# Key units by halves of the batches, and state products directly behind the second own terms, in a one-core decoder block

## The chip, the core and the metric

The kernel runs on one core of a Trainium2 chip. The metric is the device time of one launch in microseconds (us). It has five engines with an instruction stream each: TensorE (PE in the profile, with its weight loads as PEld), VectorE (DVE), ScalarE (ACT), GpSimd (POOL) and SyncE (SP, which here only issues DMAs; SPq in the profile). They are kept in step by semaphores alone: a wait in one engine's stream holds everything behind it on that engine.

## The reference

The input x has 16 sequences of 64 tokens and 256 features, all in float32, and there is a context of 16 x 64 x 128. The block is three layers, each with its residual and a LayerNorm:

```python
# 1: recurrent attention, 16 heads of 16, in 4 chunks of 16 tokens; per chunk, with state S
kh = k @ S;  v_new = gradient of a LayerNorm loss at kh
o  = q + LN(q @ S - tril(q k^T) eta v_new);  S = S - (k eta)^T v_new
x  = LN(x + (rmsnorm(o * sigmoid(gate)) * norm_w) @ Wo)
# 2: cross attention, 16 heads of 128
q = rmsnorm(x @ Wq) * gq;  k = rmsnorm(ctx @ Wk) * gk
x = LN(x + softmax(q k^T / sqrt(128)) @ (ctx @ Wv) @ Wo)
# 3: gated feed-forward with rows rounded to 8 bit
x = LN(x + quant(silu(quant(x) @ Wg) * (quant(x) @ Wu)) @ quant(Wd))
```

## The kernel before

The program has three parts in time. The first prepares weights and projections. The second is the recurrence: chunks c = 0 to 3, each in halves h = 0, 1 (a half is 8 of the 16 heads). The third is a pipeline over 8 tiles of 128 tokens that does the output projection of the recurrence, the cross attention and the feed-forward; its steps are numbered from i = -2.

**The recurrence.** For each chunk PE runs, for both halves: `state_products(c, h)` (L518, k and q times the state; it waits for `s_ready`), `scores_ttt(c, h)` (L500, q k^T within the chunk; made one chunk ahead, it waits for the masked keys `kb` and its half 1 ends with `a_done`), and `own_terms(c, h)` (L528, it waits for `ub_ready`, the update rows of that half, and for `at_ready`, the masked scores). Each is 64 matmuls of 32 rows, which the trace shows as 128 pairs of a weight load and a matmul. Below they are called state(c,h), scores(c,h) and own(c,h). DVE does in order: `state_read(c, 0)` (begins with the transpose khR, L1427), `kb_rows` and `a_masked` (ak, L1409 and L1414), the previous chunks' outputs (`output_inverse`, ors, L1525, which waits for a root osd on ACT; `out_c`), `chain(c, 0)` (some 12 small steps that end with ub, L1462), `state_read(c, 1)`, `output_sums`, `output_inverse`, `chain(c, 1)`, `out_normed`, `after_own_terms(c, 0)` (qhR, L1513, and the new state rows st, L1517, which set `s_ready`), `out_gated`, and `after_own_terms(c, 1)`. ACT takes roots (`state_root`, `output_root`, L1080), squares and the masked keys (`k_blocks`, L1013).

**The key units.** The keys of the cross attention, which need only the context, are made in between: 32 units, each one head of one half of the batches (512 columns). A unit is one float32 matmul on PE (L659, two pairs in the trace) into bank 6 or 7, a square (L1071) and a scaled copy (L1073) on ACT. After every fourth unit PE sums four squares into bank 5 (L650, `key_sum`, 8 pairs), each into one row of its own. When all 32 are summed, ACT takes one root `krow` (L1076), SP writes it to DRAM and reads it back with one row per batch and head (`roots_to_rows`, L420 and L423, both halves), DVE inverts it (`key_scales`, kinv, L1549), SP writes it (`scales_out`, L427) and reads it back as the broadcast rows `rkb` (`scale_rows(i)`, L435), with which DVE multiplies the scores of tile i (`scores_out`, pr, L1707). `rkb` lies over buffers of the key units, so it is loaded after all of them.

A unit's place is set by hand, by the numbers in `KEY_PLACES`, one list for each chunk; PE takes a number at each place between its recurrence steps, and ACT takes the same numbers in its own order:

```python
# PE, chunk c: state(c,0) keys state(c,1) keys scores(c+1,0) keys own(c,0) keys scores(c+1,1) keys own(c,1) keys
# ACT, chunk c:
keys(places[0])
if c < NCH - 1:
    k_blocks(c + 1)
keys(places[1])
output_root(2 * c - 1)
state_root(c, 1)
```

Bank 6 and 7 alternate, so unit n waits until ACT has emptied unit n - 2. Behind the last sums PE runs 8 matmuls that are not used (`warm(4, 8)`, L643) and then `ttt_out(0)` (L834), the first of the pipeline, whose result DVE reads (rw, L1757).

Of the kernel before, what the change touches and what calls it, by code (L numbers as in the profile page):

```python
# [32 lines left out]
ACT = mybir.ActivationFunctionType  # L33
# [5 lines left out]
NCH = T // C  # L39
# [16 lines left out]
KEY_PLACES = [(1, 2), (2, 2, 1, 1, 2, 1), (2, 2, 1, 1, 2, 1), (2, 3, 3, 3)]  # L56
# [3 lines left out]
def decoder_block(nc, x, ctx_in, Wq, Wk, Wv, Wo, Wbeta, ln_w, ln_b, Wg1, Wg2, norm_w,  # L60
                  XWq, XWk, XWv, XWo, gq, gk, w1_in, w2_in, out):
    stack = ExitStack()
    with stack:
# [213 lines left out]
        def unit_of(n):  # L277
            return n % 2, n // 4 * 2 + n % 4 // 2
# [100 lines left out]
        def _(sp):  # L379
# [64 lines left out]
            load_x()  # L444
            sp.wait_ge(sem("og_ready"), 2)
# [11 lines left out]
            scale_rows(1)  # L457
            scales_out(1)
# [13 lines left out]
        def _(pe):  # L472
# [372 lines left out]
            warm(4, 8)  # L845
# [3 lines left out]
            pe.wait_ge(sem("k_rooted"), 1)  # L849
# [101 lines left out]
        def _(act):  # L951
# [113 lines left out]
            def key_unit(n):  # L1065
# [8 lines left out]
                else:  # L1074
                    act.wait_ge(sem("k_summed"), NKU)
# [875 lines left out]
```

## Time and profile before

| | us |
|---|---|
| median of 3 runs | 381.57 |
| lowest and highest | 378.9, 383.26 |
| the profiled execution | 382.47 |
| its span | 380.7 |
| PE busy in the span | 344.8 (91%) |
| DVE busy | 264.5 (69%) |
| ACT busy | 201.3 (53%) |

The profiled execution is longer than its span by 1.77 us, which lies outside the first and the last instruction. Its time is 0.9 us over the median of the runs and inside their spread. In the rows of a timeline the first number is the start in us from the begin of the span, the second the time from the first to the last of the merged instructions, the bracket at the end the time that the engine was idle just before, and what released it ("issue": nothing that the profile shows).

### The profile page before, as it was taken

The numbers are of one execution on the slowest core, as the hardware profiler recorded it, in microseconds if no ns is written. First come the engines' busy times: TensorE is split into PE (matmuls) and PEld (weight loads), VectorE is DVE, ScalarE is ACT, GpSimd is POOL, SyncE is SP. The second block draws the span as 40 slices with busy tenths as digits, with TensorE's granted clock in tenths as the row PEclk, the third lists the DMA queues.
The fourth block names the chain that finished last, engine by engine and source line by source line (L and its number), as shares of the span: only waits on it lengthen the run. The fifth ranks groups of instructions, "written<-read, shape, count | busy, mean of one in ns | idle before, by whom it ended". The sixth has DMA issues, their size and how long they took to land.

```text
span 380.7 us, 11631 instructions
## 1 busy us (share of the span) xinstructions
PE 344.8 (91%) x5095; PEld 242.8 (64%) x5098; DVE 264.5 (69%) x536; ACT 201.3 (53%) x371; POOL 75.6 (20%) x91
## 2 busy tenths in 40 slices
PE   1999997998979877998999999999999999999974
PEld 1544585455435332587698796896977969866731
DVE  0499997897797899556263674855846739566795
ACT  1245974855525635255516556555555566576351
POOL 3009300000000000000062341522714505300100
PEclk9999999999987968999999999999999999999998
DMA  8997000000402001029120100200201000000000
GB/s 195 277 289 248 4 4 3 5 3 23 151 4 83 34 2 58 16 53 203 31 57 0 50 8 15 58 0 16 57 1 56 16 15 0 2 15 0 16 1 28
DMA packets 17986, 19.96 MB, mean 52 GB/s; under 512 B 3712, under 2 KB 15376, under 8 KB 17680
## 3 DMA queue, kind: packets, MB, share of 16 engines
q1 hardware_dynamic: 17328, 18.69, 18.8%
q8 instruction: 40, 0.66, 0.8%
q10 hardware_dynamic: 608, 0.54, 0.7%
q14 instruction: 10, 0.08, 0.1%
HBM read 18.04 MB, written 1.18 MB: 50 GB/s over the span
## 4 chain that ended last, share of the span: by engine, by line
PE 73%; DVE 15%; ACT 4%; issue 3%; DMA 3%; SPq 0%; POOLq 0%; POOL 0%; DVEq 0%
PE ps L790 14%; PE ps L724 12%; PE ps L547 6%; PE ps L659 5%; PE ps L782 5%; PE ps L767 4%; PE ps L500 3%; PE ps L809 2%; PE ps L528 2%; PE ps L740 2%; PE ps L518 2%; PE ps L617 2%; PE ps L650 2%; PE ps L758 2%; DMA xn<-in_x_dram 2%
## 5 line engine op out<-in xcount | busy, mean ns | idle before, releaser
L724 PEld LDWEIGHTS ps<-x1t,xwq 128*128 128x128 f32 x512 | 59.2, 192 | 6.4 <-issue 4.2
L724 PE MATMUL ps<-x1t,xwq 128*128 128x128 f32 x512 | 62.1, 278 | 0.7 <-ACT x1t L1188 0.7
L790 PE MATMUL ps<-mvo,cxp 128*128 128x256 f32 x224 | 51.8, 383 | 0.5 <-ACT cxp L1199 0.5
L1893 POOL TENSOR_SCALAR rstd<-mv 128x1 f32<-128x1 f32 x20 | 4.4, 218 | 212.6 <-DVE mv L1635 212.6
L790 PEld LDWEIGHTS ps<-mvo,cxp 128*128 128x128 f32 x224 | 41.3, 190 | 6.6 <-ACT cxp L1199 0.8
L659 PE MATMUL ps<-ctxt,xwk 128*128 128x512 f32 x64 | 39.1, 727 | 3.5 <-ACT kt L1073 2.3
L1151 ACT ACTIVATE qt<-ps 128x512 f32<-128x512 f32 x32 | 19.1, 596 | 33.9 <-PE ps L724 33.9
L1071 ACT ACTIVATE ksq<-ps 128x512 f32<-128x512 f32 x32 | 18.9, 591 | 21.4 <-PE ps L659 13.4
L1073 ACT ACTIVATE kt<-ps,gks 128x512 f32<-128x512 f32 x32 | 21.9, 683 | 0.0
L1158 ACT ACTIVATE qsq<-ps 128x512 f32<-128x512 f32 x32 | 19.0, 593 | 4.2 <-PE ps L740 4.2
L659 PEld LDWEIGHTS ps<-ctxt,xwk 128*128 128x128 f32 x64 | 11.9, 217 | 14.3 <-ACT kt L1073 6.2
L528 PEld LDWEIGHTS ps<-ak,ub 32*32 32x32 f32 x1024 | 11.9, 109 | 13.7 <-issue 13.5
L767 PEld LDWEIGHTS ps<-kt,qt 128*64 128x64 f32 x512 | 16.2, 138 | 6.8 <-ACT qt L1151 3.8
L528 PE MATMUL ps<-ak,ub 32*32 32x48 f32 (+1 forms) x1024 | 13.4, 200 | 6.9 <-DVE ub L1462 3.5
L1644 DVE TENSOR_SCALAR x<-rr,mv,rstd 128x256 f32<-128x256 f32 x16 | 6.6, 412 | 18.7 <-POOL rstd L1894 18.5
L782 PE MATMUL ps<-pt,ctx 64*128 64x512 f32 x64 | 18.5, 638 | 0.7 <-ACT pt L1178 0.7
L767 PE MATMUL ps<-kt,qt 128*64 128x64 f32 x512 | 18.4, 225 | 0.0
L1707 DVE TENSOR_TENSOR pr<-ps,rkb 128x1024 f32<-128x1024 f32 x8 | 9.8, 1224 | 12.2 <-PE ps L767 8.7
L1199 ACT ACTIVATE cxp<-ps 128x512 f32<-128x512 f32 x28 | 15.3, 606 | 4.5 <-PE ps L782 4.5
L1683 DVE TENSOR_TENSOR gs<-ps,s 128x352 f32<-128x352 f32 x16 | 8.3, 522 | 13.4 <-PE ps L809 13.2
L1908 POOL TENSOR_TENSOR rq<-rq,mhalf 128x16 f32<-128x16 f32 x6 | 17.4, 2908 | 0.5
L500 PEld LDWEIGHTS ps<-kqi,kb 32*32 32x32 f32 x1024 | 10.1, 110 | 7.8 <-issue 6.8
(238 smaller groups left out, 683.2 us busy)
## 6 DMA issues: line engine op xcount, KB each, us to landing
rkb<-kscale SPq DMA_DIRECT2D x16, 256.0 KB, 4.2
ctx<-in_ctx_dram SPq DMA_DIRECT2D x4, 512.0 KB, 8.7
xwo<-in_L_xattn_Wo_dram SPq DMA_DIRECT2D x1, 2048.0 KB, 14.2
xwq<-in_L_xattn_Wq_dram SPq DMA_DIRECT2D x4, 512.0 KB, 4.8
w1n<-in_L_ffn_w_gate_up_dram SPq DMA_DIRECT2D x1, 1408.0 KB, 9.9
xwv<-in_L_xattn_Wv_dram SPq DMA_DIRECT2D x1, 1024.0 KB, 11.2
xwk<-in_L_xattn_Wk_dram SPq DMA_DIRECT2D x1, 1024.0 KB, 16.5
xn<-in_x_dram SPq DMA_DIRECT2D x2, 512.0 KB, 5.9
```

Of the source, the lines that this page charges most:

```text
L500: last = mm(ps[part, 4 * BANK + g * C:4 * BANK + (g + 1) * C], kb[part, g * 32:(g + 1) * 32], kq[part, col:col + C], start=True, stop=True)
L528: last = mm(ps[part, g * GW + C:g * GW + C + w], ub[part, g * 32:(g + 1) * 32], ak[part, g * (C + 32):g * (C + 32) + w], start=c == 0 and ...
L547: last = mm(bank(bk), w[:, k * D + hh * P:k * D + (hh + 1) * P], xt[:, k * B * T + half * BANK:k * B * T + (half + 1) * BANK], start=k == ...
L659: mm(bank(6 + n % 2), xwk[:, h * XD:(h + 1) * XD], ctxt[:, half * BANK:(half + 1) * BANK], start=True, stop=True)\
L724: last = mm(bank(n % 2, P, t * P), xwq[qn][:, k * BANK + t * P:k * BANK + (t + 1) * P], x1t[:, (i % 2) * D + k * P:(i % 2) * D + (k + 1) * ...
L767: last = mm(ps[b2 * T:(b2 + 1) * T, 4 * BANK + h * T:4 * BANK + (h + 1) * T], qt[:, h * P + b2 * T:h * P + (b2 + 1) * T], kt[:, (i * XH + ...
L782: turn_done(mm(bank(bk), ctx2[rows, b * CD:(b + 1) * CD], pt[rows, :].rearrange("p (h q) -> p h q", q=P)[:, :, b2 * T:(b2 + 1) * T], start ...
L790: last = mm(bank(turn_banks[turn_of[("y", i, 0)]], D), context_of(i)[:, h * P:(h + 1) * P], mvo[:, h * D:(h + 1) * D], start=h == 0, stop= ...
L1071: A(ksq[n % 4][:, :], bank(6 + n % 2), ACT.Square).then_inc(sem("k_squared"), 1)
L1073: A(o, bank(6 + n % 2).rearrange("p (i t) -> p i t", t=P), ACT.Copy, scale=gks[:, 1:2]).then_inc(sem("key_emptied"), 1)
L1151: A(qt[:, qn * BANK:(qn + 1) * BANK], bank(n % 2), ACT.Copy).then_inc(sem("q_copied"), 1)
L1158: A(qsq[:, (n % 2) * BANK:(n % 2 + 1) * BANK], bank(n % 2), ACT.Square).then_inc(sem("q_squared"), 1)
```

## The change

It has four parts. The order of the key units goes from alternating halves of the batches to all 16 heads of the first half and then the second. The root is taken twice: after unit 17 for the first half, and at the end; the rows of the first half go through DRAM at a place of SP's stream behind `load_x`, their inverse is taken by DVE in the last chunk's output steps (`key_scales(0)`), and `scale_rows(0)` no longer stands behind the inverse of both. In the recurrence, scores(c,1) is moved from before own(c-1,1) to after state(c,0), own(c,1) is followed by state(c+1,0) with no unit between, and `a_masked` stands behind `out_c` on DVE. The 8 matmuls of `warm` are 3.

```diff
-KEY_PLACES = [(1, 2), (2, 2, 1, 1, 2, 1), (2, 2, 1, 1, 2, 1), (2, 3, 3, 3)]
+KEY_PLACES = [(1, 2), (1, 2, 2, 1, 3), (1, 1, 2, 1, 4), (1, 2, 2, 3, 3)]
...
         def unit_of(n):
-            return n % 2, n // 4 * 2 + n % 4 // 2
+            return divmod(n, XH)
...
             def roots_to_rows(half):
-                sp.wait_ge(sem("k_rooted"), 1)
-                for odd in range(2):
-                    at = 64 * half + 32 * odd
...
-                sp.wait_ge(sem("k_rows_out"), 32 * (half + 1))
+                sp.wait_ge(sem("k_rooted"), half + 1)
+                for q in range(4):
+                    at = 32 * q + 4 * half
...
+                sp.wait_ge(sem("k_rows_out"), 64 * (half + 1))
+                sp.wait_ge(sem("kh_done"), 4)
...
@@ key_sum
                 pe.wait_ge(sem("k_squared"), n + 1)
-                at = 31 - h // 2
+                if half == 1:
+                    pe.wait_ge(sem("k_rooted"), 1)
+                at = 31 - h // 4 - 4 * half
...
@@ PE, the loop over chunks
                 state_products(c, 0)
                 keys(next(places))
+                if c >= 2:
+                    scores_ttt(c, 1)
+                keys(next(places))
                 state_products(c, 1)
                 keys(next(places))
                 if c < NCH - 1:
                     scores_ttt(c + 1, 0)
                     keys(next(places))
                 own_terms(c, 0)
-                if c < NCH - 1:
-                    keys(next(places))
-                    scores_ttt(c + 1, 1)
                 keys(next(places))
                 own_terms(c, 1)
-                for n in places:
-                    keys(n)
+            keys(next(places))
...
-            warm(4, 8)
+            warm(4, 3)
...
-            pe.wait_ge(sem("k_rooted"), 1)
+            pe.wait_ge(sem("k_rooted"), 2)
@@ ACT, key_unit
+                if n == XH + 1:
+                    act.wait_ge(sem("k_summed"), XH)
+                    A(krow[:, :], bank(5), ACT.Sqrt, bias=eps_t[:, 1:2], scale=1.0 / XD).then_inc(sem("k_rooted"), 1)
@@ ACT, the loop over chunks
-                keys(places[0])
+                keys(places[0] + places[1])
                 if c < NCH - 1:
                     k_blocks(c + 1)
-                keys(places[1])
+                    keys(places[2] + places[3])
+                else:
+                    keys(places[2])
                 output_root(2 * c - 1)
                 state_root(c, 1)
@@ DVE
                     kb_rows(c)
-                    a_masked(c)
                     output_inverse(2 * c - 2)
                     out_c(c - 2)
+                    a_masked(c)
...
             output_sums(2 * NCH - 2)
+            key_scales(0)
             last_scale(qhR, 0)
...
                     last_out(2)
-                    key_scales()
+                    key_scales(1)
```

On PE, from own(1,0) to state(2,0), before:

```order
L528 MATMUL ps<-ak,ub 32x48 x63
L659 MATMUL ps<-ctxt,xwk 128x512 [waits key_emptied]
...
L500 MATMUL ps<-kqi,kb 32x16 x64
L659 MATMUL ps<-ctxt,xwk 128x512 [waits key_emptied] x2
L528 MATMUL ps<-ak,ub 32x48 [waits ub_ready,kbr_ready,at_ready]
L528 MATMUL ps<-ak,ub 32x48 x63
L659 MATMUL ps<-ctxt,xwk 128x512 [waits key_emptied]
L518 MATMUL ps<-kqi,st 32x64 [waits s_ready]
```

and in the changed kernel (own terms are L529 there, units L663, state products L519, scores L501, sums L653):

```order
L529 MATMUL ps<-ak,ub 32x48 x63
L663 MATMUL ps<-ctxt,xwk 128x512 [waits key_emptied] x3
L529 MATMUL ps<-ak,ub 32x48 [waits ub_ready,kbr_ready,at_ready]
L529 MATMUL ps<-ak,ub 32x48 x63
L519 MATMUL ps<-kqi,st 32x64 [waits s_ready]
L519 MATMUL ps<-kqi,st 32x64 x63
```

The 64 score matmuls of half 1 and the unit ahead of the state products are gone from here; the scores stand behind state(2,0) and unit 12 now, and in chunk 1 the sums of units 4 to 7 stand before own(1,0).

On ACT, chunk 1 from the masked keys to the roots osd and sdc that DVE waits for (each pair of ksq and kt is a unit), before, units 5 and 6:

```order
L1013 ACTIVATE kb<-kqi,mask_h 128x32x16
L1071 ACTIVATE ksq_130<-ps 128x512 [waits k_summed,key_done]
L1073 ACTIVATE kt<-ps,gks 128x4x128
L1071 ACTIVATE ksq_131<-ps 128x512 [waits k_summed,key_done]
L1073 ACTIVATE kt<-ps,gks 128x4x128
L1080 ACTIVATE osd<-ovs,eps_t 128x32 [waits ovs_ready]
```

and in the changed kernel, units 6, 7 and 8 (squares L1074, copies L1076, roots L1087):

```order
L1016 ACTIVATE kb<-kqi,mask_h 128x32x16
L1074 ACTIVATE ksq_131<-ps 128x512 [waits k_summed,key_done]
L1076 ACTIVATE kt<-ps,gks 128x4x128
L1074 ACTIVATE ksq_74<-ps 128x512 [waits k_summed,key_done]
L1076 ACTIVATE kt<-ps,gks 128x4x128
L1074 ACTIVATE ksq_129<-ps 128x512 [waits k_summed,key_done]
L1076 ACTIVATE kt<-ps,gks 128x4x128
L1087 ACTIVATE osd<-ovs,eps_t 128x32 [waits ovs_ready]
```

The roots of chunk 1 stand behind unit 8 where they stood behind unit 6; those of chunk 2 stand behind unit 16 where they stood behind unit 15.

On SP, from the last weight load to the second half's rows, before:

```order
L381 DMA xwq_160<-in_L_xattn_Wq_dram 128x2x512 [waits mg_done]
L420 DMA kroot<-krow 8x8x64 [waits k_rooted]
...
L423 DMA kinv<-kroot 128x64 [waits k_rows_out]
L427 DMA kscale<-kinv 128x64 [waits k_inverted,k_summed]
L435 DMA rkb<-kscale 64x1024 [waits k_scales_out]
L435 DMA rkb<-kscale 64x1024
L381 DMA ctx_58<-in_ctx_dram 64x16x128 x2
L435 DMA rkb<-kscale 64x1024 [waits k_scales_out]
L435 DMA rkb<-kscale 64x1024
L427 DMA kscale<-kinv 128x64 [waits k_inverted]
```

and in the changed kernel:

```order
L428 DMA kscale<-kinv 128x64 [waits k_inverted]
L436 DMA rkb<-kscale 64x1024 [waits k_scales_out,k_summed]
L436 DMA rkb<-kscale 64x1024
L381 DMA ctx_58<-in_ctx_dram 64x16x128 x2
L436 DMA rkb<-kscale 64x1024 [waits k_scales_out]
L436 DMA rkb<-kscale 64x1024
L420 DMA kroot<-krow 4x8x64 [waits k_rooted]
L420 DMA kroot<-krow 4x8x64 x3
L424 DMA kinv<-kroot 128x64 [waits kh_done,k_rows_out]
L428 DMA kscale<-kinv 128x64 [waits k_inverted]
```

The second half's rows go out and come back behind the loads of rkb for tiles 0 and 1 and of the context, where before they went ahead of them.

## Rows read from the trace of the kernel before

**Rows 1.** Busy time by stretches: from:to, length, then each engine's busy us, clock, DMA

```profile
100.00:120.00 20.00, 17.55 (x613) 10.20 (x616) 18.31 (x48) 9.96 (x20) 0.00 (x0) 0.83 0.02 4
...
240.00:280.00 40.00, 40.00 (x340) 34.12 (x340) 27.81 (x54) 23.08 (x40) 17.66 (x16) 1.00 0.12 31
```

**Rows 2.** Timeline of DVE, chunk 1 and the start of chunk 2

```profile
82.08 0.35 DVE L1525 RECIPROCAL ors<-osd 128x32 f32<-128x32 f32 x1 [0.39 <-ACT osd L1080]
...
87.96 0.48 DVE L1462 TENSOR_SCALAR ub<-us__111,mask_h 128x128 f32<-128x128 f32 x2
...
93.25 0.45 DVE L1513 STREAM_TRANSPOSE qhR<-ps 128x256 f32<-128x256 f32 x1 [1.68 <-PE ps L528]
...
97.25 0.45 DVE L1427 STREAM_TRANSPOSE khR<-ps 128x256 f32<-128x256 f32 x1 [2.23 <-PE ps L518]
```

**Rows 3.** Timeline of PE, chunks 1 and 2

```profile
75.85 1.99 PE L518 MATMUL ps<-kqi,st 32*32 32x64 f32 x128
77.77 1.98 PE L659 MATMUL ps<-ctxt,xwk 128*128 128x512 f32 x4
79.68 1.26 PE L500 MATMUL ps<-kqi,kb 32*32 32x16 f32 x128
...
91.31 1.82 PE L528 MATMUL ps<-ak,ub 32*32 32x48 f32 x128
...
96.77 0.42 PE L518 MATMUL ps<-kqi,st 32*32 32x64 f32 x15 [0.85 <-issue]
...
105.97 0.44 PE L500 MATMUL ps<-kqi,kb 32*32 32x16 f32 x31 [0.63 <-issue]
...
111.34 0.71 PE L528 MATMUL ps<-ak,ub 32*32 32x48 f32 x42 [1.82 <-issue]
111.98 2.08 PE L659 MATMUL ps<-ctxt,xwk 128*128 128x512 f32 x2
```

**Rows 4.** Table of the costliest groups: the two ACT operations of a key unit

```profile
L1071 ACT ACTIVATE ksq<-ps 128x512 f32<-128x512 f32 x32 | 18.9, 591 | 21.4 <-PE ps L659 13.4
L1073 ACT ACTIVATE kt<-ps,gks 128x512 f32<-128x512 f32 x32 | 21.9, 683 | 0.0
```

**Rows 5.** Timeline of DVE, chunk 2 and the start of chunk 3

```profile
110.18 0.35 DVE L1525 RECIPROCAL ors<-osd 128x32 f32<-128x32 f32 x1 [0.39 <-ACT osd L1080]
...
120.83 0.45 DVE L1513 STREAM_TRANSPOSE qhR<-ps 128x256 f32<-128x256 f32 x1 [1.16 <-PE ps L528]
...
124.70 0.45 DVE L1427 STREAM_TRANSPOSE khR<-ps 128x256 f32<-128x256 f32 x1 [2.10 <-PE ps L518]
```

**Rows 6.** Timeline of ACT and PE behind the last sums

```profile
153.62 0.69 ACT L1076 ACTIVATE krow<-ps,eps_t 128x512 f32<-128x512 f32 x1 [0.77 <-PE ps L650]
...
155.26 1.89 PE L834 MATMUL ps<-wo,ogt 128*128 128x256 f32 x8
```

**Rows 7.** Timeline of the first scores: inverse, loads, scores, root table, exponential

```profile
165.69 0.91 DVE L1549 RECIPROCAL kinv<-kinv 128x128 f32<-128x128 f32 x1
...
168.16 1.12 SPq L435 DMA_DIRECT2D rkb<-kscale  x2
...
170.71 3.63 SPq L435 DMA_DIRECT2D rkb<-kscale  x2
171.09 1.15 PE L767 MATMUL ps<-kt,qt 128*64 128x64 f32 x32
...
173.15 1.23 DVE L1707 TENSOR_TENSOR pr<-ps,rkb 128x1024 f32<-128x1024 f32 x1 [3.56 <-DMA rkb<-kscale]
...
176.72 1.28 ACT L1208 ACT_TABLE_LOAD   x1
...
178.41 1.06 ACT L1208 ACTIVATE pr<-pr 128x1024 f32<-128x1024 f32 x1 [0.40 <-DVE pr L1718]
```

**Rows 8.** Lines 427 (stores kscale<-kinv) and 423 (loads kinv<-kroot): time to landing

```profile
DMA to landing us min/median/max: 1.5/4.9/8.3
...
DMA to landing us min/median/max: 1.8/2.5/3.1
```

More of the change, by code:

```diff
@@ L416, in roots_to_rows @@
             def roots_to_rows(half):
-                sp.wait_ge(sem("k_rooted"), 1)
-                for odd in range(2):
-                    at = 64 * half + 32 * odd
-                    sp.dma_start(kroot[half].rearrange("b (r o) t -> o r b t", o=2)[odd],
-                                 krow[at:at + XH // 2, :].rearrange("p (b t) -> p b t", t=T)).then_inc(sem("k_rows_out"), 16)
-                sp.wait_ge(sem("k_rows_out"), 32 * (half + 1))
-                sp.dma_start(kinv[:, half * T:(half + 1) * T], kroot[half].rearrange("b h t -> (b h) t")).then_inc(sem("k_roots_in"), 16)
+                sp.wait_ge(sem("k_rooted"), half + 1)
+                for q in range(4):
+                    at = 32 * q + 4 * half
+                    sp.dma_start(kroot[half].rearrange("b (r o) t -> o r b t", o=4)[q],
+                                 krow[at:at + 4, :].rearrange("p (b t) -> p b t", t=T)).then_inc(sem("k_rows_out"), 16)
+                sp.wait_ge(sem("k_rows_out"), 64 * (half + 1))
+                sp.wait_ge(sem("kh_done"), 4)
+                sp.dma_start(kinv[:, half * T:(half + 1) * T], kroot[half].rearrange("b h t -> (b h) t")).then_inc(sem("k_roots_in%d" % half), 16)
             def scales_out(half):
-                sp.wait_ge(sem("k_inverted"), 1)
+                sp.wait_ge(sem("k_inverted"), half + 1)
                 sp.dma_start(kscale[half * B // 2:(half + 1) * B // 2, :].rearrange("b (h t) -> (b h) t", t=T),
@@ L444, in _ @@
             load_x()
+            roots_to_rows(0)
             sp.wait_ge(sem("og_ready"), 2)
@@ L457, in _ @@
             scale_rows(1)
+            roots_to_rows(1)
             scales_out(1)
@@ L646, in key_sum @@
                 half, h = unit_of(n)
-                rows = slice(64 * half + 32 * (h % 2), 64 * half + 32 * (h % 2) + 32)
+                rows = slice(32 * (h % 4), 32 * (h % 4) + 32)
                 pe.wait_ge(sem("k_squared"), n + 1)
-                at = 31 - h // 2
-                mm(bank(5)[rows, :], onehot[:, at:at + 32], ksq[n % 4][:, :], start=h < 2, stop=h >= XH - 2).then_inc(sem("k_summed"), 1)
+                if half == 1:
+                    pe.wait_ge(sem("k_rooted"), 1)
+                at = 31 - h // 4 - 4 * half
+                mm(bank(5)[rows, :], onehot[:, at:at + 32], ksq[n % 4][:, :], start=n < 4, stop=n >= NKU - 4,
+                   skip_group_check=True).then_inc(sem("k_summed"), 1)
             def key_unit(n):
@@ L1116, in _ @@
                 output_square(c - 1)
-                keys(places[0])
+                keys(places[0] + places[1])
                 if c < NCH - 1:
                     k_blocks(c + 1)
-                keys(places[1])
+                    keys(places[2] + places[3])
+                else:
+                    keys(places[2])
                 output_root(2 * c - 1)
                 state_root(c, 1)
-                for n in places[2:-2]:
-                    keys(n)
-                keys(places[-2])
+                keys(places[4] if c < NCH - 1 else places[3])
                 gated_square(c - 1)
-                if c < NCH - 1:
-                    keys(places[-1])
             last_root(0)
@@ L1545, in out_c, with key_scales @@
                 V.transpose(o, oR[:, :]).then_inc(sem("o_feat"), 1)
-            def key_scales():
-                dve.wait_ge(sem("k_roots_in"), 32)
-                V.reciprocal(kinv[:, :], kinv[:, :]).then_inc(sem("k_inverted"), 1)
+            def key_scales(half):
+                own = kinv[:, half * T:(half + 1) * T]
+                dve.wait_ge(sem("k_roots_in%d" % half), 16)
+                V.reciprocal(own, own).then_inc(sem("k_inverted"), 1)
             kb_rows(0)
```

7 lines of the change are left out of this document (3 added, 4 removed).

## The prediction

> **What bounds the kernel now.** I read the busy times by stretches first, then the timeline of DVE through the recurrence, then PE's around every point at which DVE was idle. From 200 us on PE is busy all the time (40.00 of 40 us), and nothing of the change is there; what it can move lies before. In the recurrence no engine is full: in 100 to 120 us DVE has 18.31 us of work and PE 17.55, at a granted clock of 0.83 of full [rows 1]. The steps of DVE are one behind another, so I take DVE's stream as the path, and PE counts where DVE waits for it. Such waits stand twice in each of chunks 1 and 2: for own(c,1) 1.68 and 1.16 us, and for the next state(c+1,0) 2.23 and 2.10 us [rows 2, 5]. Together 7.2 us, and the most that the new order can give there.
>
> **PE's stops.** PE waits also for nothing that the profile shows: 0.85, 0.63 and 1.82 us in the middle of a group [rows 3]. Counting the pairs of a weight load and a matmul between the first two stops (the last 15 of state(2,0), unit 12 with sums, unit 13, state(2,1), units 14 and 15, 97 of scores(3,0)) gives 15 + 2 + 8 + 2 + 128 + 4 + 97 = 256; to the third it is 127. So the places are marks every 128 pairs, and PE stops where it reaches one too soon. The mark before 96.77 lies 116 pairs into own(1,1), by its row at 91.31 + 0.9 x 1.82 = 92.95 us; my estimate is thus 3.8 us from mark to mark, with 5.4 (105.97 to 111.34) as the other end. The new order puts own(c,1) and state(c+1,0) together, 256 pairs in a row that could otherwise run in some 3.8 us: it must meet a stop. The Trainium skill, "Runtime: NRT & Kernel Launch", section "Instruction fetch mechanics", says that instructions come in blocks of 256 and that such a crossing is "mostly hidden". The spacing agrees (128 pairs are 256 instructions), the cost does not: by that sentence the sum below would be 0.6 us better.
>
> **Chunk 1.** ACT's order costs. Its roots osd and sdc stand behind unit 8 now, and PE reaches that only after unit 5, state(1,1), units 6 and 7 and scores(2,0). From 75.85 us, where state(1,1) began, that is 4 units at 1.0 (two took 1.98), 1.92 and 1.2 for the others [rows 3]: 83.0. ACT's square and copy (0.59 and 0.68 [rows 4]) and the root bring DVE's ors to about 84.6, where it stood at 82.08 [rows 2]: **2.6 us later**. All behind it moves along. The last ub ends at 91.0 (88.44 before), DVE would be free for own(1,1) at 94.15 (93.25 - 1.68 + 2.6), and own(1,1) is done by then (91.0 + 1.8): the wait of 1.68 is gone. DVE then needs 1.8 more (from 93.25 to 97.25 less the idle 2.23), to 96.0. State(2,0) could start at 92.9, when the rows of half 0 are written, but its mark lies 114 pairs in, and the one before it at 92.5; with 3.8 that gives 96.3, and 0.1 for the rest. So state(2,0) is read at **96.5 instead of 97.25**, 0.75 earlier; ends: 0 with a longer stop, 1.2 with none. The exchanged places of `a_masked` and `out_c` cost nothing as long as scores(2,1), now behind state(2,0), unit 12 and sums, ends by 100.9; I get 100.2, a margin of 0.7.
>
> **Chunk 2.** From 96.6 PE has units 12 to 16 (5.2), sums (1.0), scores(2,1), state(2,1), scores(3,0) (1.25, 2.0, 1.25) and three short stops by my marks (1.6) before ACT can finish unit 16: 108.9, so ors at 110.5 against 110.18 [rows 5], **0.3 later**. DVE reaches `after_own_terms(2, 1)` at 120.0 (120.83 - 1.16 + 0.3). Own(2,0), from 110.0 to 111.8, four units and sums bring PE to 117.1, own(2,1) ends at 118.7, so that wait of 1.16 is gone too; DVE is done with its steps at 121.8. State(3,0) starts at 118.8; its mark lies 72 pairs in, and the one before it at 118.0: with 3.8 that is 121.8, and 56 pairs more make 122.4, **2.3 us before 124.70**. If PE's clock falls in units 17 to 20, they take 2.08 each instead of 1.05 [rows 3], own(2,1) ends at 121.8 and state(3,0) at 125.4: 0.7 late. Before, the clock was down there after a stop of 1.82; now units and sums stand before own(2,0), so I hold it the less likely. For the recurrence I take **-1.8**, nearer to 2.3. Chunk 3 is DVE's work alone, in the same order, and gives nothing.
>
> **Behind the recurrence.** `key_scales(0)` adds half of 0.91 to DVE, behind the sums that ACT's next root needs, and lies beside PE's last unit: nothing, or 0.5 if that cover is gone. The root of the first half on ACT (0.69) stands between units, beside DVE's chain: nothing. PE's new wait on `k_rooted` has that root behind unit 17 and is asked behind unit 20: nothing. Three of `warm` instead of 8: the last sums end at 153.6, `krow` at 154.31, and `ttt_out(0)` begins at 155.3 [rows 6], so the 8 take 1.7; three would take 0.7 and end level with `krow`, whose root is waited for in both kernels. **-1.0**. Its other end: clock. The units before it ran at half clock, and with fewer matmuls ahead `ttt_out(0)` may run at it, 1.9 us for its four instead of 0.95. I charge half, **+0.4**.
>
> **The scales.** DVE waited for rkb until 173.15, but the scores themselves end at 172.24 [rows 7], so 0.9 can come free. ACT then cannot begin the exponential before its table is loaded, at 178.0, against 178.41: 0.4 remain. Against that stands the second half: its rows leave behind rkb for two tiles and the context, 2 MB, and DVE waits for them in `key_scales(1)`, ahead of the first scores. Before, the same queue held SP in one issue for 3.63 us [rows 7], and a 32 KB store behind it landed after 8.3 us instead of 1.5 [rows 8]. Counted from the end of the last sums (T), SP issues the rows at T + 6.3 if the issues ahead take as long as before (168.16 to 174.34 [rows 7]). They land between T + 7.8 (1.5 later, an empty queue) and T + 14.6 (8.3 later), and the read back takes 1.8 to 3.1 [rows 8]. So kinv is there between T + 9.6 and T + 17.7; with 2 MB queued I expect the upper half. The half inverse (0.5) and DVE's steps for tile 2 (2.6, an estimate from five small operations of some 0.4 and a trip to POOL) follow, and the scores are ready at T + 17.6 (172.24 - 153.6 - 1.0). Up to T + 14.5 it costs nothing, at the upper end 3.2. I take **-0.2**.
>
> **Sum.** -1.8 - 1.0 + 0.4 - 0.2 = -2.6. The profiled execution's 382.47 would be 379.9; from the median of 381.57 it is **379.0 us**. A measurement of this kernel can tell about 1%, 3.8 us, from no change (its three runs span 4.4).
>
> **Rivals.** (1) PE keeps its full clock and stops little: the recurrence gives 2.8, `warm` 1.0, the scales 0.4, and the last unit and sums, which ran at half clock (a unit then takes 2.08), give back up to 2.0: 375.4 to 377.4. For it: units now fill PE's idle time before own(3,0). Against: with DVE as the path, PE waits before own(1,1) and own(3,1) instead, 2 us or more each, as long as the idle times after which the clock fell. (2) The clock falls in the wrong places: recurrence +0.7, `warm` -0.1, scales 0: 382.2. For it: the idle 2.1 us before own(1,1) that ACT's order makes. (3) Slower: the second half's rows through a full DMA queue. It decides from kinv at T + 14.5; to be slower than before in all it must come after T + 16.9; at T + 17.7 with the rest as forecast it is 382.5, and with both ends of the clock 384 to 386. For it: the 8.3 us landing; against: nothing more is queued behind the rows now, as SP waits for them.
>
> **How the numbers follow.** Forecast (377.8 to 380.6) 0.52; rival 1 0.24; rival 2 0.12; rival 3 0.12. Faster by over 1% is below 377.75: rival 1 and a tenth of the forecast, 0.30. Slower by over 1% is above 385.4: half of rival 3, 0.07. Range 375.4 to 383.0, which leaves out the far end of rival 1 and rival 3's upper part.
>
> **What would show it.** DVE's ors in chunk 1 near 84.6 with some 3 us of idle time ahead of it, put down to ACT; DVE's idle time ahead of qhR of half 1 gone, ahead of khR below 0.6, with PE stopped on issue inside state(2,0) and state(3,0); khR of chunk 3 at 122.4; `ttt_out(0)` 0.8 us behind the last sums instead of 1.8; the first pr no longer waiting for rkb, and kinv of the second half with or without a wait for its DMA. Wrong would be the forecast if ACT is ready before unit 8 is waited for, if the marks are not a matter of time between them, or if the rows land later than T + 14.6.

## Result and the profile after

The changed kernel takes **387.62 us** (median of 4 runs, 385.42 to 388.89) against 380.31 us for the kernel before (median of 4 runs; the 381.57 that the forecast started from was the median of 3 of them): a ratio of 1.0176, with a 95% interval of 1.0093 to 1.0259. The range of the prediction was 375.4 to 383.0 us, so the time lies outside it, on the slow side. The profiled execution has a span of 386.0 us, 5.3 us more than before. The medians are 7.3 us apart: the profiled execution of the kernel before was 2.2 us above its median, that of the changed kernel is at its own. Some executions are slower throughout at a lower granted clock (one of e5 took 420 us, one of e1 564 us); all ratios are of the others.

DVE's timeline, chunks 1 to 3 of the changed kernel (answers to rows 2 and 5; the same columns):

```profile
85.49 0.35 DVE L1530 RECIPROCAL ors<-osd 128x32 f32<-128x32 f32 x1 [3.85 <-ACT osd L1087]
...
96.31 0.45 DVE L1518 STREAM_TRANSPOSE qhR<-ps 128x256 f32<-128x256 f32 x1 [1.34 <-PE ps L529]
99.85 0.45 DVE L1432 STREAM_TRANSPOSE khR<-ps 128x256 f32<-128x256 f32 x1 [1.77 <-PE ps L519]
...
105.75 0.69 DVE L1419 TENSOR_TENSOR ak<-ps,tri 128x512 f32<-128x512 f32 x1 [1.68 <-PE ps L501]
...
116.89 0.35 DVE L1530 RECIPROCAL ors<-osd 128x32 f32<-128x32 f32 x1 [2.71 <-ACT osd L1087]
...
126.41 0.45 DVE L1518 STREAM_TRANSPOSE qhR<-ps 128x256 f32<-128x256 f32 x1
128.10 0.44 DVE L1432 STREAM_TRANSPOSE khR<-ps 128x256 f32<-128x256 f32 x1
...
134.35 0.69 DVE L1419 TENSOR_TENSOR ak<-ps,tri 128x512 f32<-128x512 f32 x1 [2.04 <-PE ps L501]
...
144.44 0.35 DVE L1530 RECIPROCAL ors<-osd 128x32 f32<-128x32 f32 x1 [1.65 <-ACT osd L1087]
```

In chunk 2 the waits for own(2,1) and state(3,0) are gone (126.41, 128.10), as the change could hope for. But each chunk has a wait for the root osd, 3.85, 2.71 and 1.65 us, where the kernel before has 0.39 in all three ([rows 2, 5] show two of them), and chunks 2 and 3 have one for the masked scores (ak) that no row of before shows.

ACT's timeline around the root in chunks 1 and 2 (answers to rows 4):

```profile
84.07 0.60 ACT L1074 ACTIVATE ksq<-ps 128x512 f32<-128x512 f32 x1 [1.90 <-PE ps L653]
84.56 0.68 ACT L1076 ACTIVATE kt<-ps,gks 128x512 f32<-128x512 f32 x1
85.13 0.32 ACT L1087 ACTIVATE osd<-ovs,eps_t 128x32 f32<-128x32 f32 x1
...
115.47 0.60 ACT L1074 ACTIVATE ksq<-ps 128x512 f32<-128x512 f32 x1 [1.92 <-PE ps L653]
115.97 0.68 ACT L1076 ACTIVATE kt<-ps,gks 128x512 f32<-128x512 f32 x1
116.54 0.32 ACT L1087 ACTIVATE osd<-ovs,eps_t 128x32 f32<-128x32 f32 x1
```

The square ahead of the root does not wait for its unit (L663) but for the sums (L653). There are four buffers for squares, so the square of unit n waits until n - 3 units are summed; for n = 8, 16 and 24 these sums stand on PE *behind that very unit*. So the root hears of everything on PE up to there.

PE's timeline, unit 8 and its sums, then the stops (answers to rows 3):

```profile
81.87 1.13 PE L663 MATMUL ps<-ctxt,xwk 128*128 128x512 f32 x2
82.93 1.07 PE L653 MATMUL ps<-ksq,onehot 128*32 128x512 f32 x8
...
87.03 0.29 PE L529 MATMUL ps<-ak,ub 32*32 32x48 f32 x8 [1.63 <-issue]
...
91.99 1.39 PE L529 MATMUL ps<-ak,ub 32*32 32x48 f32 x113 [1.22 <-DVE ub L1467]
95.64 0.46 PE L529 MATMUL ps<-ak,ub 32*32 32x48 f32 x12 [2.26 <-issue]
...
99.37 0.42 PE L519 MATMUL ps<-kqi,st 32*32 32x64 f32 x15 [0.37 <-issue]
...
101.78 1.04 PE L501 MATMUL ps<-kqi,kb 32*32 32x16 f32 x103
105.29 0.40 PE L501 MATMUL ps<-kqi,kb 32*32 32x16 f32 x25 [2.47 <-issue]
...
127.32 0.72 PE L519 MATMUL ps<-kqi,st 32*32 32x32 f32 x60 [1.41 <-issue]
...
133.24 1.04 PE L501 MATMUL ps<-kqi,kb 32*32 32x16 f32 x62 [3.47 <-issue]
```

From 99.37 to 105.29 and from 127.32 to 133.24 are 5.9 us each from mark to mark, 128 pairs apart (15 + 2 + 8 + 103, and 60 + 2 + 66). The rows with "<-issue" begin at marks, that is where the next block of 128 pairs begins. The DMA queues say why these two are long. Queue 8 is marked as carrying instructions, in packets of 16 KB: it has 40 of them in the whole span, and PE's 10,186 records (matmuls and weight loads) are 39.8 times 256. Four windows of the changed kernel, 99.4 to 102.9, 102.9 to 103.2, 127.4 to 130.6 and 130.6 to 131.2 us; the columns are packets, MB and the share of 16 engines:

```profile
q1 hardware_dynamic: 962, 0.96, 89.0%
...
q1 hardware_dynamic: 31, 0.03, 25.9%
q8 instruction: 1, 0.02, 23.3%
...
q1 hardware_dynamic: 433, 0.85, 80.5%
...
q1 hardware_dynamic: 97, 0.18, 77.1%
q8 instruction: 1, 0.02, 9.4%
```

Behind both marks queue 1 (the loads of Wq and x on SP, 1.5 MB from 97.4 to 104.6 us and 1 MB from 127.6 to 131.7) fills the engines, and the instruction packet starts only late in the load, at 102.9 and 131.0; PE goes on 2.4 and 2.3 us behind that. In the kernel before, one packet (at 99.5 us) came at the end of the first load, too, but units and sums lay between it and the next mark, and no stop shows there.

Behind the recurrence (answers to rows 6 and 7; ACT, PE, DVE):

```profile
160.62 0.69 ACT L1083 ACTIVATE krow<-ps,eps_t 128x512 f32<-128x512 f32 x1 [1.11 <-PE ps L653]
...
161.56 1.97 PE L837 MATMUL ps<-wo,ogt 128*128 128x256 f32 x8 [0.23 <-ACT krow L1083]
...
175.35 0.55 DVE L1555 RECIPROCAL kinv<-kinv 128x64 f32<-128x64 f32 x1 [3.20 <-DMA kinv<-kroot]
...
178.73 1.23 DVE L1714 TENSOR_TENSOR pr<-ps,rkb 128x1024 f32<-128x1024 f32 x1 [0.38 <-PE ps L770]
...
184.40 1.06 ACT L1213 ACTIVATE pr<-pr 128x1024 f32<-128x1024 f32 x1
```

The account of the 5.3 us: from khR(1,0) to the end of the last sums it is 88.5 us instead of 81.5 (+7.0); from there to the first rw 2.2 instead of 2.8 (-0.6); from rw to the exponential 21.6 instead of 22.0 (-0.4); the rest of the pipeline is 0.7 us shorter, with no row of its own to it.

The clock has a part in the 7.0 that no run separates. Behind the stops of 2.26, 2.47 and 3.47 us PE runs at the lower of its two levels (granted clock 0.55, 0.50 and 0.50, that is about 1.2 GHz), so that unit 13 takes 2.08 us instead of 1.12 and units 22 and 23 take 3.78 instead of 1.98; behind those of 1.63 and 1.41 it was at 1.00.

### The profile page after: what moved, and what is told of

Read it like the earlier page. It is cut to its first block, busy times and chain, and to the rows that moved or that the text cites. A ratio compares the mean times of both kernels' runs of the same rounds, so it can differ in the third digit from the quotient of the medians.

```text
span 386.0 us, 11649 instructions
## 1 busy us (share of the span) xinstructions
PE 343.7 (89%) x5093; PEld 242.5 (63%) x5093; DVE 264.5 (69%) x537; ACT 201.9 (52%) x372; POOL 75.7 (20%) x91
## 4 chain that ended last, share of the span: by engine, by line
PE 75%; DVE 12%; ACT 6%; issue 4%; DMA 2%; SPq 0%; POOLq 0%; POOL 0%; DVEq 0%
PE ps L727 15%; PE ps L793 14%; PE ps L548 6%; PE ps L663 5%; PE ps L770 4%; PE ps L785 4%; PE ps L519 3%; PE ps L501 3%; PE ps L812 2%; PE ps L743 2%; PE ps L653 2%; PE ps L618 2%; PE ps L837 2%; PE ps L761 2%; DMA xn<-in_x_dram 2%
## 5 line engine op out<-in xcount | busy, mean ns | idle before, releaser
L663 PE MATMUL ps<-ctxt,xwk 128*128 128x512 f32 x64 | 37.0, 686 | 5.2 <-ACT kt L1076 4.0
L1074 ACT ACTIVATE ksq<-ps 128x512 f32<-128x512 f32 x32 | 19.0, 594 | 25.9 <-PE ps L663 16.8
L1076 ACT ACTIVATE kt<-ps,gks 128x512 f32<-128x512 f32 x32 | 22.0, 687 | 0.0
L663 PEld LDWEIGHTS ps<-ctxt,xwk 128*128 128x128 f32 x64 | 11.0, 200 | 16.9 <-ACT kt L1076 9.5
L529 PEld LDWEIGHTS ps<-ak,ub 32*32 32x32 f32 x1024 | 11.4, 105 | 15.5 <-issue 15.5
L529 PE MATMUL ps<-ak,ub 32*32 32x48 f32 (+1 forms) x1024 | 12.9, 197 | 8.9 <-issue 5.3
L519 PEld LDWEIGHTS ps<-kqi,st 32*32 32x32 f32 x768 | 12.6, 126 | 6.8 <-issue 6.5
L501 PEld LDWEIGHTS ps<-kqi,kb 32*32 32x32 f32 x1024 | 9.8, 107 | 11.1 <-issue 10.1
```

The costliest lines, as they stand in the source:

```text
L501: last = mm(ps[part, 4 * BANK + g * C:4 * BANK + (g + 1) * C], kb[part, g * 32:(g + 1) * 32], kq[part, col:col + C], start=True, stop=True)
L519: last = mm(out, st[part, g * 32:(g + 1) * 32], moving, start=g % (BANK // GW) == 0, stop=False, skip_group_check=True)
L529: last = mm(ps[part, g * GW + C:g * GW + C + w], ub[part, g * 32:(g + 1) * 32], ak[part, g * (C + 32):g * (C + 32) + w], start=c == 0 and ...
L663: mm(bank(6 + n % 2), xwk[:, h * XD:(h + 1) * XD], ctxt[:, half * BANK:(half + 1) * BANK], start=True, stop=True)\
L1074: A(ksq[n % 4][:, :], bank(6 + n % 2), ACT.Square).then_inc(sem("k_squared"), 1)
L1076: A(o, bank(6 + n % 2).rearrange("p (i t) -> p i t", t=P), ACT.Copy, scale=gks[:, 1:2]).then_inc(sem("key_emptied"), 1)
```

## Experiments

Each experiment's ratio is against executions of the kernel before on the same chip; e3, e5, e8, g1 and g3 have only 3 or 4 executions. "Path" is the time from khR(1,0) to the first rw in the run's profile; "osd" and "ak" are DVE's waits of chunks 1 to 3 for the root and the masked scores, summed.

| run | ratio to before, 95% interval | path | osd | ak |
|---|---|---|---|---|
| before | 1 | 84.3 | 1.2 | 0 |
| changed | 1.0176 [1.0093, 1.0259] | 90.7 | 8.2 | 3.7 |
| e5 order alone | 1.0167 [1.0099, 1.0236] | 90.2 | 7.6 | 3.1 |
| e4 scales alone | 0.9954 [0.9919, 0.9988] | 84.1 | 1.2 | 0 |
| e1 roots ahead | 1.0024 [0.9992, 1.0056] | | | |
| e1b the same | 0.9991 [0.9952, 1.0031] | 84.4 | 1.6 | 0.9 |
| e7 roots ahead, chunk 1 | 1.0030 [0.9994, 1.0066] | 86.4 | 4.0 | 2.9 |
| e3 roots, scores back | 1.0214 [1.0149, 1.0278] | 94.7 | 1.6 | 0 |
| e8 marks moved | 1.0226 [1.0146, 1.0306] | 89.5 | 7.7 | 2.8 |
| d1 before, loads late | 0.9943 [0.9904, 0.9981] | 83.1 | 1.2 | 0 |
| d2 changed, loads late | 0.9981 [0.9957, 1.0005] | 84.6 | 6.6 | 0 |
| g3 second load late | 1.0107 [1.0053, 1.0161] | 86.1 | 7.0 | 1.4 |
| d3 roots ahead, loads late | 0.9938 [0.9913, 0.9963] | 82.5 | 1.6 | 0 |
| g1 d3, scores back | 1.0114 [1.0048, 1.0179] | 88.0 | 1.6 | 0 |
| g2 d3, 8 matmuls | 0.9971 [0.9938, 1.0004] | 83.2 | 1.6 | 0 |
| e6 scales, 3 matmuls | 0.9978 [0.9938, 1.0018] | 87.1 | 1.2 | 0 |
| d4 e6, loads late | 0.9905 [0.9865, 0.9946] | 80.9 | 1.2 | 0 |

### Which half of the change loses: e5 and e4

e5 is the kernel before with the new order of the recurrence alone (the lists of units, PE's and ACT's loops, `a_masked` behind `out_c`); e4 is the kernel before with the rest but for `warm` (units and scales by halves).

> The kernel before with the new order of the recurrence alone (unit places, scores(c,1) behind state(c,0), no unit ahead of state(c+1,0), ACT's order); units by alternating halves, one root, the scales at the end and 8 warm matmuls as before. Theory A (the recurrence's new order costs: DVE waits for roots that stand on ACT behind units 8, 16, 24, whose squares wait for sums, and for masked scores that PE now makes on DVE's path): the first read of chunk 3's state, which came 3.4 us late in the changed kernel, is 3.4 late here too and the last sums end 7 us late; 386 to 389. Theory C (the halves of the scales cost, by their transfers and the second root): no slower than 382.

> The kernel before with the units and scales by halves alone (two roots, the first half through DRAM during chunk 3's run-up, second half behind the loads of rkb); recurrence order and 8 warm matmuls as before. Theory A: within 1 us of before, 379.5 to 381.5, with DVE waiting some 3 us for kinv of the second half without effect on the first scores. Theory C: 3 us or more slower than before.

Measured: 1.0167 and 0.9954. The order carries the whole loss. The scales win half a per cent in the order of before; with the new order (1.0176 with them and the shorter warm-up, 1.0167 without) nothing of it shows. In e4's profile 0.4 us of it stand between rw and the exponential (21.6 against 22.0) and 0.1 in the path; the rest has no row of its own. The wait for the second half's rows, 2.70 us there, did not hold up the first scores: DVE waited 0.88 us for these themselves.

### The roots' place: e1, e1b, e7

```diff
@@ ACT, the loop over chunks (e1, e1b)
-                    keys(places[2] + places[3])
-                else:
                     keys(places[2])
                 output_root(2 * c - 1)
                 state_root(c, 1)
-                keys(places[4] if c < NCH - 1 else places[3])
+                keys(places[3] + places[4] if c < NCH - 1 else places[2] + places[3])
```

> The changed kernel with one thing undone on ACT: the roots osd and sdc of chunks 1, 2 and 3 stand ahead of units 8, 16 and 24 again. Theory A1 (the roots' place is the larger part; it added 3.4, 2.3 and 1.3 us to DVE's waits): DVE's waits for osd fall to 0.4, the last sums come 3 to 6 us earlier, 381 to 384. Theory A2 (PE's stops and the late scores bind, the roots only hid them): above 385.5, with the waits for osd short and DVE's idle time moved to khR, qhR or the masked scores.

> The changed kernel with the two roots of each chunk ahead of units 8, 16 and 24 on ACT, once more, since the profile of the first such run cannot be read for times (its executions gave a ratio of 1.0024). Theory A1 (the roots are late because the square ahead of them waits for the sums that PE does behind that unit): DVE's waits for osd fall from 3.85, 2.71 and 1.65 us to under 1 us in all three chunks, the last sums end 4 to 6 us earlier than in the changed kernel, and the whole takes 381 to 383 us. Theory A2 (the masked scores behind PE's stops are the loss): ak still waits for PE for 1.5 to 2 us in chunks 2 and 3, and the time does not fall by more than 2 us from that of the changed kernel. What is left of the order's loss against the kernel before should then stand as waits for scores and state products.

> The changed kernel with the roots ahead of the unit on ACT in chunk 1 alone (chunks 2 and 3 as changed). A1 says that each chunk adds its own part: ors of chunk 1 comes 3 to 3.5 us earlier than the changed kernel's 85.5, the waits of chunks 2 and 3 (2.7 and 1.7 us) stay, and 2 to 3.5 us of the 5.5 us are won: 384 to 386 us. The rival is that a lead won in chunk 1 is lost again at the next stop of PE or at the next root, since these are tied to PE's row of instructions: then 386.5 to 388 us, no different from the changed kernel.

Measured: 1.0024 and 0.9991, so 1.5 to 1.9% is won by moving two small roots ahead of one unit (ahead of two, 24 and 25, in chunk 3; of e1 only the times are used). With the roots ahead in chunk 1 alone the ratio is 1.0030 already, and the path is 4.3 us shorter, where the three chunks give 6.3: more than chunk 1's own wait (3.07 us less) explains. DVE's waits of e1b, chunks 1 and 2:

```profile
81.42 0.35 DVE L1528 RECIPROCAL ors<-osd 128x32 f32<-128x32 f32 x1 [0.78 <-ACT osd L1087]
...
100.87 0.69 DVE L1417 TENSOR_TENSOR ak<-ps,tri 128x512 f32<-128x512 f32 x1 [0.85 <-PE ps L501]
...
109.69 0.35 DVE L1528 RECIPROCAL ors<-osd 128x32 f32<-128x32 f32 x1 [0.39 <-ACT osd L1087]
```

The roots are a cause. But the wait for the scores has fallen as well, from 1.68 to 0.85 us in chunk 2 and from 2.04 to nothing in chunk 3, though nothing of theirs was changed; that points to a second cause that depends on when things run.

### Whose stops they are: e8

```diff
@@ PE, ahead of unit 0
+            for _ in range(64):
+                mm(bank(4)[0:32, 0:16], ident_b[0:32, 0:32], ident_b[0:32, 0:16], start=True, stop=True)
```

> The changed kernel with 64 small matmuls (64 pairs of a weight load and a matmul, 32 x 16, results unused) in PE's idle time ahead of unit 0. They cost nothing by themselves (PE waits there for 1.19 us). If PE's stops belong to fixed counts of its instructions (a mark after every 128 pairs), every stop falls 64 pairs earlier in the program than in the changed kernel: the stops in the middle of scores(2,1), state(3,0) and scores(3,1) (at 105.29, 127.32 and 133.24) move to other steps, and the time changes by as much as the stops then cost DVE, between 3 us less and 2 us more. If the stops belong to the steps themselves (a port or a memory conflict of these matmuls), they stay at the same places in the steps and the time stays within 1 us of 387.6.

```profile
103.69 0.93 PE L501 MATMUL ps<-kqi,kb 32*32 32x16 f32 x89 [1.78 <-issue]
...
125.30 1.25 PE L519 MATMUL ps<-kqi,st 32*32 32x32 f32 x124 [1.47 <-issue]
...
130.67 1.90 PE L501 MATMUL ps<-kqi,kb 32*32 32x16 f32 x126 [1.98 <-issue]
```

These are PE's rows of e8. Scores(2,1), state(3,0) and scores(3,1) stop 39, 4 and 2 pairs in, where the changed kernel stopped 103, 68 and 66 pairs in: all three moved by exactly 64. The stops belong to the count of instructions, not to the matmuls that they hit. The 64 were not free (khR(1,0) starts 1.2 us later), the path is 1.2 us shorter, and the whole is no faster (1.0226).

### The loads: d1, d2, g3, d3

```diff
@@ SP (d1; in d2 and d3 roots_to_rows(0) stands ahead of the first added line; g3 has only the second)
             sp.wait_ge(sem("mg_done"), 2 * 2)
+            sp.wait_ge(sem("k_summed"), 24)
             load_xwq(0)
             load_x()
             sp.wait_ge(sem("og_ready"), 2)
+            sp.wait_ge(sem("k_summed"), 28)
             load_xwq(1)
```

> The kernel before with one change on SP: the load of the first piece of Wq and of x (1.5 MB together, at 94 to 100 us before) waits until 24 key units are summed, and the next two pieces (1 MB, at 121 to 126 us) until 28 are. Theory F: PE's instructions come in 16 KB packets on a DMA queue of their own, and a packet that is due while those loads run starts only near their end; in the trace of before a packet starts at 99.42 inside the load of 94.13 to 99.95 us, in the changed kernel at 103.03 and 131.11 inside loads of 97.38 to 104.64 and 127.56 to 131.66 us, and PE stops until 2.3 to 2.7 us behind each. With the loads later, no packet between 90 and 130 us starts more than 2 us after the mark ahead of it, PE's stops there fall under 1 us, and the kernel takes 2 to 4 us less than before: 377.5 to 380 us. Rival: the packets are late for another reason (PE's own waits), the stops stay, and the time is within 1 us of before.

> The changed kernel with the same delay of the loads on SP (the first half's roots stay ahead of them). Theory F: the stops of 2.47 us in scores(2,1) and of 1.41 and 3.47 us in state(3,0) and scores(3,1) shrink to under 1 us each, ak's waits for PE with them, and 2 to 4 us are won; the waits for osd behind units 8, 16 and 24 (3.9, 2.7, 1.7 us) stay or grow by what is won ahead of them: 383.5 to 386 us. Rival: the recurrence's path is then bound by the roots alone and nothing is won: 387 to 388 us.

> The changed kernel with only the second load on SP (two pieces of Wq, 1 MB, at 127.6 to 131.7 us) later, until 28 units are summed; the first (1.5 MB at 97.4 to 104.6 us) stays. Both together later gave 0.9981 against 1.0176. If each load costs by the packet that it holds up, the stop of 2.5 us in scores(2,1) stays, those of 1.4 and 3.5 us at 127 and 133 us fall to 0.4 to 1.7 us, and about 3 us are won: 384 to 385 us. Rival: what is won after the first load is lost to the roots of chunk 3, 387 us.

> The changed kernel with both repairs: the roots of each chunk ahead of units 8, 16 and 24 on ACT, and the loads on SP later. If the roots' place (5 to 6 us) and the instruction packets behind the loads (2 to 4 us) are the two things that the changed order lost by, this is faster than the kernel before: 376 to 379 us. If the order has a loss of its own beside these (the scores of half 1 on DVE's path, own(c,1) and state(c+1,0) as 256 pairs in a row), it stays at 380 to 382 us.

For the packet starts in the first of these texts the traces give 99.5, 102.9 and 131.0 us; its argument stays the same.

Measured: the kernel before gains 0.6% (0.9943). Its packets start 1.0 to 1.1 us behind PE's going on, but a stop of 2.14 us stays between 90 and 130 us (and one of 1.54 at 87.8), with no load near, against what I expected; the path is 1.1 us shorter, and I can't put down the rest of the gain to single stops. The changed kernel gains 1.9% (1.0176 to 0.9981), 7.4 us where 2 to 4 were expected. PE's rows of d2 at the marks of above, then queue 8 from 99.9 to 101 us:

```profile
95.64 0.46 PE L531 MATMUL ps<-ak,ub 32*32 32x48 f32 x12 [1.00 <-issue]
...
99.36 0.42 PE L521 MATMUL ps<-kqi,st 32*32 32x64 f32 x15 [0.20 <-issue]
...
125.07 0.72 PE L521 MATMUL ps<-kqi,st 32*32 32x32 f32 x60 [1.68 <-issue]
...
128.52 1.04 PE L503 MATMUL ps<-kqi,kb 32*32 32x16 f32 x62 [0.43 <-issue]
```

```profile
q8 instruction: 1, 0.02, 5.3%
```

Behind the mark at 99.36 the packet starts at 100.5 instead of 102.9, scores(2,1) runs through without a stop (2.47 before the move), and scores(3,1) stops for 0.43 us instead of 3.47; from mark to mark it is 3.5 us there instead of 5.9. DVE no longer waits for ak, and its waits for osd shrank too, in chunks 2 and 3:

```profile
85.75 0.35 DVE L1532 RECIPROCAL ors<-osd 128x32 f32<-128x32 f32 x1 [3.86 <-ACT osd L1089]
...
114.35 0.35 DVE L1532 RECIPROCAL ors<-osd 128x32 f32<-128x32 f32 x1 [1.97 <-ACT osd L1089]
...
139.15 0.35 DVE L1532 RECIPROCAL ors<-osd 128x32 f32<-128x32 f32 x1 [0.78 <-ACT osd L1089]
```

This fits the fact that either repair wins nearly all and both together only 2.4% (d3, 0.9938): a root that hears of PE's whole row passes PE's stops on to DVE, so the two costs are in part the same microseconds (0.74 and 0.87 us of the waits for osd here). d2 against d3 gives what the roots' place costs without the loads: 0.4%, or 2.1 us of path. g3 divides the loads: with only the second moved away, the stop in scores(2,1) stays (2.20 us), that in scores(3,1) falls to 1.28, the one in state(3,0) stays at 1.59, and 0.7% is won. State(3,0)'s stop was the same with and without a load near it (1.41, 1.59 and 1.68 us in the changed kernel, g3 and d2). The path says otherwise: of 6.1 us that both loads cost, 4.6 go with the second alone moved, three quarters where the times show a third. The path is that of one execution, the fastest of g3's four (382.3 us; two took 385.0 and 385.3), so how the cost divides between the two loads stays open.

### The scores behind own terms, and the warm-up: e3, g1, g2

e3 is e1 with `scores_ttt(c + 1, 1)` back between `own_terms(c, 0)` and `own_terms(c, 1)`, but directly behind the first, where the kernel before has units between (and none behind `state_products(c, 0)`); g1 is the same with the loads late; g2 is d3 with `warm(4, 8)`.

> The changed kernel with the roots ahead of units 8, 16 and 24 and scores(c+1,1) back behind own(c,0), a chunk ahead of their use, but still no unit between own(c,1) and state(c+1,0). Theory A1: both costs gone, the gains at the chunk boundaries (1 to 2 us each) stay, 377 to 380. Theory A2: the four 128-pair groups scores, own, state in a row meet PE's stops and the boundary comes no earlier than before; 380 to 383.

> The changed kernel with the roots ahead of units 8, 16 and 24, the loads later, and the scores of half 1 back ahead of own(c,1) (directly behind own(c,0)). With the loads in their old place the same return of the scores cost 1.9% (0.9991 and 1.0024 without it, 1.0214 with it). If that was the packets behind the loads, it now costs under 0.5%: 379 to 381 us. If a row of scores, own terms and state products without enough units in it stops PE by itself, the waits of DVE for own(c,1) and state(c+1,0) stay at 4 to 6 us and the time is 384 us or more.

> The changed kernel with the roots ahead and the loads later, and 8 instead of 3 unused matmuls behind the last sums: the price of the warm-up by itself. From krow to the first result read was 2.5 us shorter only by 0.7 us in the changed kernel; the same here: 0.5 to 1.0 us more than with 3 (379.4), 380 to 380.5 us. Rival: the clock of the pipeline's first tiles profits from the 5 matmuls more, and the time is the same or less.

e3 was a surprise (1.0214), and g1 refutes my explanation of it by the loads: 1.0114 where d3 has 0.9938, so the return of the scores costs 1.8% with the loads away and 1.9 to 2.2% with them. PE and one window of g1 (columns as in rows 1):

```profile
87.10 1.21 PE L503 MATMUL ps<-kqi,kb 32*32 32x16 f32 x120
90.72 0.31 PE L503 MATMUL ps<-kqi,kb 32*32 32x16 f32 x8 [2.41 <-issue]
90.96 5.42 PE L665 MATMUL ps<-ctxt,xwk 128*128 128x512 f32 x6
```

```profile
90.70:96.40 5.70, 5.68 (x22) 2.04 (x26) 1.96 (x3) 2.35 (x4) 0.00 (x0) 0.52 0.01 3
```

Own terms and scores are 256 pairs without a unit between, as own(c,1) and state(c+1,0) are: PE stops 2.41 us with no load near. Behind the stop the granted clock is 0.52 of full, the lower of its two levels (1.2 GHz), and three units take 5.42 us instead of 3. DVE then waits 5.59 us for own(1,1). So once own(c,1) and state(c+1,0) are joined, scores directly behind own(c,0) are the wrong place; behind state(c,0) they cost 1.8% less. The place of before, with a unit between own(c,0) and the scores, was not run with the joined groups.

g2 gives the warm-up's price: from the last sums to rw 2.80 us with 8 and 2.19 with 3, in the times 0.33%, with intervals that overlap.

### A version that beats both: e6 and d4

e6 is e4 with `warm(4, 3)`; d4 is e6 with the loads late. The recurrence's order is that of before.

> The kernel before with the units and scales by halves and with 3 instead of 8 unused matmuls behind the last sums; the order of the recurrence as before, roots and scores too. The halves alone gave 0.9954 of the time before. The warm-up part: 5 matmuls of 0.38 us between krow and the first output product, so that the first result is read 0.7 to 1 us earlier, if the root krow is not later: 0.9930 to 0.9945, 378.7 to 379.6 us. Rival: the three matmuls leave TensorE at its low clock at the begin of the pipeline, or krow is what the output product waits for: then no less than 0.9954.

> The kernel before, its recurrence order unchanged, with the units and scales by halves, 3 unused matmuls and the loads on SP later. The waits of DVE for own(1,1) (3.9 us) and for state(3,0) (4.2 us), which stood in this order behind stops of PE of up to 3.0 us, fall to 1 to 2 us each: 376.5 to 379 us. If theory F is wrong: 380.5 to 381 us as without the delay.

e6 is at 0.9978, no better than e4 (0.9954), against the 0.9930 to 0.9945 expected; the intervals overlap. Its profiled execution, 2.1 us above its median, has a stop of 3.01 us in state(2,1) at 105.38 us behind a packet that came at 102.9, at the end of the first load (95.2 to 102.9). With the loads away (d4) it is **0.9905 [0.9865, 0.9946], 378.3 us**, the lowest ratio of all, without the new order; d3, with that order repaired, is at 0.9938, and the intervals of the two overlap.

## Why the prediction was wrong

The forecast was 2.6 us faster; the times are 7.3 us slower, the profiles 5.3. The steps that failed are the stops of PE (each put at 3.8 us from mark to mark), the margin of 0.7 us for the masked scores, and "gives nothing" for chunk 3; the root in chunks 1 and 2 was rightly named and sized too small.

**Chunk 1, the roots** (ors at 84.6, khR(2,0) at 96.5). The mechanism was right and undersized by 0.9 us: ors came at 85.49. The step counted PE up to the end of unit 8, 83.0, which is where it came (81.87 + 1.13), then ACT's square; the square waits for the sums behind unit 8 as well, 1.07 us. The second half of the step failed: khR(2,0) came at 99.85, not 96.5. DVE waited 1.34 us for own(1,1), which the forecast had as gone, and 1.77 for state(2,0), where below 0.6 was forecast. Own(1,1) has a mark 116 pairs in. The forecast let PE run over it at 92.5; PE stopped there for 2.26 us, until 95.64, and the next mark, in state(2,0), followed 3.7 us later.

**The marks, "3.8 from mark to mark".** Where PE runs on it holds: 3.7 and 3.5 us in d2 with no load near. It failed in two ways. From 87.03 to 95.64 it was 8.6 us: PE stood 14 pairs behind the mark and waited for ub until 91.99, and the next packet started only at 92.95, 0.96 us after it went on. The same order gives the same distance in e5, d2 and g3: 0.95 to 0.96 us behind the end of that wait. So time in which PE waits there does not count towards the 3.8; that is what these four traces suggest, and no run varied it by itself. And with a load in the way it was 5.9. The other end that I had noted (5.4) was never put into the sum. In the trace of before its packet starts at 109.15, 3.2 us behind the mark at 105.97, with no load and no wait of PE that the profile shows; why is open.

**The masked scores, "a margin of 0.7".** This failed outright: scores(2,1) ended at 105.7, 5.5 us later than my 100.2 where khR(2,0) was only 3.4 later, and DVE waited 1.68 and 2.04 us. The change put a PE group on DVE's path in two chunks, and I covered it with a margin smaller than two of the three stops of [rows 3] (0.85 and 1.82).

**Chunk 2** (ors at 110.5, khR(3,0) at 122.4): 116.89 and 128.10. What it inherited is 3.4 us from chunk 1 and the 1.68 of ak; most of the other 1.4 is unit 16, whose square waits for the sums behind it (1.07), as in chunk 1. The gain at the chunk's end was right: own(2,1) and state(3,0) are not waited for. But own(2,1) itself ended only at 125.0 us (118.7 forecast); DVE was later still.

**Chunk 3, "DVE's work alone, in the same order, and gives nothing"**: it cost 3.4 us more, by the same two waits (2.04 and 1.65). The premise was wrong by the change itself: here, too, ak stands behind `out_c` and waits for scores that PE now makes behind state(3,0), and the root stands behind units 24 and 25, the first of which waits for sums.

**Behind the recurrence.** The two terms for the warm-up, -1.0 and +0.4, came out at -0.6 together, by luck: the shorter warm-up gave 0.6 by itself, as `ttt_out(0)` waited for `krow` and began 0.98 us behind the last sums instead of 1.67, and the clock cost nothing. That term rested on a misreading of [rows 6]. The 1.89 us of `ttt_out(0)` before were taken as the time at half clock; the granted clock over that row is 1.00, and over the 1.97 us of the changed kernel too, so 1.9 us is its time at full clock. The first scores gave 0.8 at pr and 0.4 at the exponential, where I had 0.9 free and 0.4 left and took 0.2 of it. The slower rival was the wrong one: kinv came 14.8 us behind the last sums, at its bound of 14.5, and its wait of 3.20 us cost nothing, since DVE then still waited 0.38 us for the scores themselves.

**The sum** was -1.8 for the recurrence; it measured +7.0. None of the rivals had the roots and the marks going wrong together. Rule and trace on the blocks of instructions: the spacing agrees in every run, "mostly hidden" (the Trainium skill, "Runtime: NRT & Kernel Launch", section "Instruction fetch mechanics") does not: the rows of the changed kernel and [rows 3] hold six stops of 1.4 to 3.5 us. That section would have made the sum 0.6 us better; the measurement decides against it.

## What to carry to other kernels

Before a small operation that another engine waits for is put behind a larger one, read all semaphores of the larger one, those for its buffers too: here a square waited for sums that stood behind its own unit. Where a stream of many small matmuls stops for nothing that the profile shows, look at the instruction queue among the DMA queues, and at what bulk loads run then: moving two loads to a stretch with large matmuls was worth 0.6% in one order and 1.9% in another. And two repairs that each win nearly all of a loss may act on the same microseconds; run both together before their gains are added.

## What the runs showed of the hardware

An instruction packet of 16 KB starts 1.1 us behind the mark where no load runs (99.36 to 100.47 in d2) and 3.5 us behind it under a load at 89% of the DMA engines (99.37 to 102.91 in the changed kernel); PE goes on 2.3 to 2.7 us after the packet's start (seven stops of the changed kernel). By which resource the load holds it up (an engine's ring or the memory) no run tells. After a stop of 2.4 us in a stream of 32-row matmuls the clock stayed at the lower level (granted clock 0.52 in g1) for 5.4 us of full-size units.
